# A convolution kernel with a new order of its first two groups and of its transition, and copies of k's rows in four parts

## The chip, the cores and the metric

The kernel runs on one core of one Trainium2 chip. The metric is the device time of one execution in microseconds; 356.31 us is the median of three runs of the kernel before (354.74 to 356.72).

## The reference, cut to what matters

For each of 32 batches there is an x of 64 heads and 1024 steps. Stage one makes for each head a kernel of 1024 taps out of 64 complex exponentials, convolves the masked x with it causally, adds a skip term and adds the result to x. Stage two multiplies each batch by the 1024 x 1024 matrix of its own adapter (ids 3 to 7) and adds that too.

```python
P = dtA[:, :, None] * jnp.arange(length)
K = 2.0 * jnp.einsum('hn,hnl->hl', Cs, jnp.exp(P)).real
...
y = irfft(rfft(u_m, n=2*L) * rfft(K, n=2*L))[..., :L] + u_m * D[:, None]
x = x + y * mask[:, None, :]
w = weight[adapter_ids]
x = x + jnp.einsum('bsi,boi->bso', x, w)
```

## The kernel before, in words

The heads form 8 groups of 8; a group has 4 pairs. For each group g:
- VectorE makes angles (`angles`), ScalarE their sines (`sines`), VectorE multiplies them with magnitudes (`factors`), ScalarE swaps halves (`exchange`), GpSimd makes `left` (`left_factor`), and TensorE multiplies it out to the group's k (`k_rows_made`). `k_high` on ScalarE and `k_low` on VectorE split k into two 16-bit parts, and ScalarE's queue stores them as `k_row` (`store_k`, 32 KB).
- SP copies each row of `k_row` 32 times with padding into `k_padded` (`copy_rows`, 1152 KB a group; in group 0 `copy_first_rows`, 288 KB a pair), and reads from there, shifted by one step per partition, two strips of 512 KB for each pair (`load_strips`). A pair's strips may be loaded when the pair one group before has been convolved.
- For x, ScalarE sums magnitudes (`sum_x`), TensorE adds them over partitions (`sum_x_bound`), VectorE makes a power of two (`x_scales`), and ScalarE and VectorE make two 16-bit parts (`x_high`, `x_low`).
- TensorE convolves a pair in two halves of 24 matmuls (`convolve`, L1135); between the halves it may do a group's `k_rows_made`. VectorE scales and masks the result into `mid` (`mask_pair`), GpSimd adds it to z (`add_masked`). `mid` holds two pairs.

A slot of stage two is up to two batches with one adapter: z_hi and z_lo of both, w_hi and w_lo of the adapter in four quarters. For the first slot SP loads the quarters behind the last strips, GpSimd adds the identity (`add_identity`, L509), ScalarE makes w_hi (L656), VectorE w_lo (L1022), each quarter by quarter; TensorE multiplies in `first_slot` (L1201), later slots at L1235. Between the last pair and `first_slot` lies the transition: the last pairs' results must be in z_hi and z_lo first (`high_parts`, `low_parts`, and a short way of its own for the last pair).

The order of work on each engine is written out by hand: groups 0 and 1 straight, groups 2 to 4 in a loop, then the rest. Each engine works through its list in order and waits on semaphores (`k_stored`, `k_copied`, `conv_done`, `masked`, `added` and so on); SP's list is the order of the transfers too.

## Time and profile before

| | us |
|---|---|
| median of 3 runs | 356.31 |
| the profiled execution | 354.95 |
| its span | 353.2 |
| TensorE busy, matmuls | 310.4 (88%) |
| VectorE busy | 215.2 (61%) |
| ScalarE busy | 151.7 (43%) |
| GpSimd busy | 118.7 (34%) |
| mean of the DMA rate over the span | 231 GB/s |

The profile is of one execution. Its times start at the first instruction; between its span and its time lie 1.8 us. A row of the timeline merges like instructions that follow each other, and the count of matmuls can be twice that of the program where data are plain f32. PE is TensorE, DVE VectorE, ACT ScalarE, POOL GpSimd; SPq is SP's queue. The granted clock is 1.00 but for stretches after idle times of TensorE.

### The profile page before, as it was taken

The page shows a single profiled execution, that of the slowest core. Times are in us where ns is not written, and L with a number is a line of the kernel's source. Part 1 is how long each engine was busy: PE and PEld are TensorE (multiplying, and loading weights), DVE is VectorE, ACT ScalarE, POOL GpSimd, SP SyncE. Part 2 cuts the span into 40 slices and gives each one's busy share as a digit, 9 for nine tenths or more (in the row PEclk, how much of TensorE's full clock was granted, in tenths as well). Part 3 has the DMA queues.
Part 4 walks back from the last instruction along what each step waited for, and adds up shares of the span by engine and source line. Part 5 has one row for each costly group of instructions (what it writes and reads, how often), then busy time and mean ns, then how long its engine had stood idle before and what let it go on. Part 6 is the DMA issues. An engine that isn't in the chain of part 4 may idle for free.

```text
span 353.2 us, 8212 instructions
## 1 busy us (share of the span) xinstructions
PE 310.4 (88%) x2604; PEld 272.7 (77%) x2605; DVE 215.2 (61%) x352; ACT 151.7 (43%) x210; POOL 118.7 (34%) x133
## 2 busy tenths in 40 slices
PE   0049789499999999977999999999999999999993
PEld 0049679498989999976888888888888888888882
DVE  5979987559889667669637740963312873196200
ACT  1956474824346501037508532653331753473200
POOL 4022665346596662565005301810001600250000
PEclk9999999969999999998999999999999999999999
DMA  7986899969999999991187038612227623932222
GB/s 260 354 367 187 320 350 392 398 248 337 376 368 389 401 366 405 399 415 50 24 307 267 0 90 312 226 27 62 59 59 291 243 59 77 401 116 59 59 60 61
DMA packets 20602, 81.60 MB, mean 231 GB/s; under 512 B 4512, under 2 KB 4704, under 8 KB 16992
## 3 DMA queue, kind: packets, MB, share of 16 engines
q1 hardware_dynamic: 18320, 80.98, 62.6%
q10 hardware_dynamic: 2256, 0.30, 0.5%
q8 instruction: 14, 0.23, 0.2%
q14 instruction: 12, 0.10, 0.1%
HBM read 72.58 MB, written 18.64 MB: 258 GB/s over the span
## 4 chain that ended last, share of the span: by engine, by line
PE 70%; DVE 15%; DMA 5%; issue 4%; ACT 3%; DVEq 1%; SPq 0%; ACTq 0%
PE bank L1235 49%; PE bank L1135 15%; PE bank L1201 4%; DMA strips<-k_padded 3%; ACT magnitude L592 2%; DMA k_row<-k_tile 2%; DVE turns L766 2%; DVE mid L842 1%; DVE phase L767 1%; DVE phase L760 1%; PE bank L1116 1%; DVE factor L778 1%; DVE z_lo L1027 1%; DVE scratch L729 1%; DMA small<-in_params 1%
## 5 line engine op out<-in xcount | busy, mean ns | idle before, releaser
L1135 PE MATMUL bank<-x,strips 128*128 (+8 forms) x1536 | 102.4, 228 | 2.1 <-DMA strips<-k_padded 2.1
L1135 PEld LDWEIGHTS bank<-x,strips 128*128 128x128 f16 x1536 | 98.4, 99 | 5.6 <-DMA strips<-k_padded 1.8
L509 POOL TENSOR_TENSOR w_raw<-w_raw,ident 128x128 f32<-128x128 f32 x40 | 40.4, 1033 | 118.5 <-DMA w_raw<-in_w 105.6
L1235 PE MATMUL bank<-w_hi,z_lo 128*128 128x512 f32 x256 | 78.8, 389 | 0.0
L1235 PE MATMUL bank<-w_hi,z_hi 128*128 128x512 f32 x256 | 78.8, 389 | 0.0
L1235 PE MATMUL bank<-w_lo,z_hi 128*128 128x512 f32 x256 | 78.7, 389 | 0.0
L487 POOL TENSOR_TENSOR z<-z,mid 128x512 f32 (+1 forms) x31 | 46.3, 1505 | 41.6 <-DVE mid L842 41.5
L1027 DVE TENSOR_TENSOR z_lo<-z,z_hi 128x512 fp32r<-128x512 f32 (+2 forms) x36 | 37.2, 1073 | 34.6 <-ACT z_hi L661 34.5
L1235 PEld LDWEIGHTS bank<-w_hi,z_hi 128*128 128x128 f32 x256 | 48.0, 188 | 10.0
L1235 PEld LDWEIGHTS bank<-w_hi,z_lo 128*128 128x128 f32 x256 | 48.0, 188 | 10.0
L1235 PEld LDWEIGHTS bank<-w_lo,z_hi 128*128 128x128 f32 x256 | 48.0, 188 | 9.9
L1022 DVE TENSOR_TENSOR w_lo<-w_raw,w_hi 128x2048 fp32r<-128x2048 f32 x20 | 48.0, 2448 | 4.7 <-ACT w_hi L656 4.7
L661 ACT CAST z_hi<-z 128x512 fp32r (+2 forms) x36 | 36.9, 1073 | 31.7 <-PE bank L1135 16.8
L656 ACT CAST w_hi<-w_raw 128x2048 fp32r<-128x2048 f32 x20 | 37.8, 1910 | 16.2 <-POOL w_raw L509 8.7
L679 ACT COPY o_tile<-bank 128x512 f32<-128x512 f32 x16 | 9.4, 585 | 72.6 <-PE bank L1235 69.1
L1042 DVE COPY o_tile<-bank 128x512 f32<-128x512 f32 x16 | 11.0, 689 | 45.8 <-PE bank L1235 44.6
L842 DVE SCALAR_TENSOR_TENSOR mid<-bank,small,mask 128x256 f32<-128x256 f32 x64 | 27.4, 475 | 16.4 <-PE bank L1135 14.5
L1146 PE MATMUL bank<-small,ones 128*128 128x4 f32 x16 | 3.4, 283 | 25.9 <-ACT magnitude L592 25.9
L601 ACT ACTIVATE x<-z,small 128x2048 f16<-128x2048 f32 (+1 forms) x8 | 16.0, 2001 | 18.7 <-PE bank L1135 14.5
L471 POOL COPY skip_row<-small 1x8 f32<-1x8 f32 (+1 forms) x8 | 12.7, 1587 | 32.5 <-DVE factor L778 32.5
L1146 PEld LDWEIGHTS bank<-small,ones 128*128 128x128 f32 x16 | 2.8, 219 | 26.1 <-issue 20.9
L829 DVE SCALAR_TENSOR_TENSOR x<-z,small,x 128x2048 f16<-128x2048 f32 (+1 forms) x8 | 21.8, 2729 | 1.2 <-ACT x L601 1.2
(175 smaller groups left out, 220.3 us busy)
## 6 DMA issues: line engine op xcount, KB each, us to landing
strips<-k_padded SPq DMA_DIRECT2D x64, 512.0 KB, 6.9
w_raw<-in_w SPq DMA_DIRECT2D x20, 1024.0 KB, 8.6
out<-o_tile SPq DMA_DIRECT2D x34, 256.0 KB
z<-in_x SPq DMA_DIRECT2D x8, 1024.0 KB, 5.4
k_padded<-k_row SPq DMA_DIRECT2D x7, 1152.0 KB, 8.3
k_padded<-k_row SPq DMA_DIRECT2D x4, 288.0 KB, 3.9
k_row<-k_tile ACTq DMA_DIRECT2D x8, 32.0 KB, 6.7
small<-in_params SPq DMA_DIRECT2D x1, 192.0 KB, 2.5
```

What stands on the lines that cost most here:

```text
L487: nc.gpsimd.tensor_tensor(z_pair[:, bass.ds(n, 1)].rearrange("p o e n -> p (o e n)"), z_pair[:, bass.ds(n, 1)].rearrange("p o e n -> p (o ...
L509: nc.gpsimd.tensor_tensor(diagonal, diagonal, ident[:, :], ALU.add).then_inc(diag_ready, 1)
L601: nc.scalar.activation(x16[:, bass.ds(g % 2, 1), 0, :].rearrange("p o n -> p (o n)"), z_group[:, bass.ds(g, 1), :].rearrange("p o n -> p ( ...
L656: nc.scalar.copy(w_hi[:, cs, :].rearrange("p c n -> p (c n)"), raw(q).rearrange("p c n -> p (c n)")).then_inc(w_hi_ready, 1)
L661: nc.scalar.copy(z_hi[:, par, :, j * H + channels.start:j * H + channels.stop], z_hcb[:, :, channels, bass.ds(b[j], 1)].rearrange("p c h o ...
L829: v.scalar_tensor_tensor(buffer[:, 1, :], z_group[:, bass.ds(g, 1), :].rearrange("p o n -> p (o n)"), x_scale[:, bass.ds(g, 1)], buffer[:, ...
L842: v.scalar_tensor_tensor(mid[:, k % 2, e, :], conv_ps[k][:, e * COL:(e + 1) * COL], xk_inverse[:, bass.ds(2 * n + e, 1)], mask[:, :, :].re ...
L1022: v.tensor_tensor(w_lo[:, cs, :], raw(q), w_hi[:, cs, :].bitcast(f32), ALU.subtract).then_inc(w_lo_ready, 1)
L1027: v.tensor_tensor(z_lo[:, par, :, j * H + channels.start:j * H + channels.stop], z_hcb[:, :, channels, bass.ds(b[j], 1)].rearrange("p c h ...
L1135: last = mm(conv_ps[k][:, e * COL + d * B:(e + 1) * COL], strips16[:, k, e, k_part, d, :], x16[:, bass.ds(g % 2, 1), x_part, col:col + (NB ...
L1201: last = mm(slot_ps[0][half][:, :], left_[:, 0, c, :], right[:, c, half * HALF:(half + 1) * HALF], start=(start and c == CQ * q and left_ ...
L1235: last = mm(slot_ps[par][half][:, :], left_[:, par, c, :], right[:, c, half * HALF:(half + 1) * HALF], start=(c == 0 and left_ is z_hi and ...
```

## The change

In groups 0 and 1 the work of TensorE, ScalarE, VectorE and SP comes in another order. k's rows of each group are copied in four parts, one for each pair, and from group 2 on each part stands behind the strips of the same pair of the group before. Two activations of one column each are added on ScalarE, which load the table of the sine. The four instructions on the adapter ids move behind the loop on VectorE. In the transition the last pair but one takes the short way too (`split_late`), GpSimd adds the identity to the first quarter before it adds pair (7,2), TensorE multiplies nine times with `ident` before the first slot, and takes w_lo of the third quarter before w_hi of the fourth.

```diff
@@ -60,7 +60,7 @@
...
     F_B0, F_B1, F_FIRST, F_ADAPTER, F_TWO, F_ACTIVE, F_NUMBER, F_ODD = range(FIELDS)
-    WARM_START, WARM_SECOND = 26, 16
+    WARM_START, WARM_SECOND, WARM_MIDDLE = 26, 16, 9
     PEEL = 4
...
     SCALED = 3
@@ -317,25 +317,18 @@
...
-            def copy_rows(g):
+            def copy_rows_of_pair(g, k):
                 sp.wait_ge(k_stored, 16 * (g + 1))
-                sp.dma_start(k_dram[g * GH:(g + 1) * GH].rearrange("h q n -> q h n"),
-                             k_row[g * GH:(g + 1) * GH].unsqueeze(0).to_broadcast([COPIES, GH, KROW])
-                             ).then_inc(k_copied, 16)
-
-            def copy_first_rows(k):
-
-                sp.wait_ge(k_stored, 16)
-                sp.dma_start(k_dram[2 * k:2 * k + 2].rearrange("h q n -> q h n"),
-                             k_row[2 * k:2 * k + 2].unsqueeze(0).to_broadcast([COPIES, 2, KROW])
-                             ).then_inc(first_copied[k], 16)
+                h = g * GH + 2 * k
+                sp.dma_start(k_dram[h:h + 2].rearrange("h q n -> q h n"),
+                             k_row[h:h + 2].unsqueeze(0).to_broadcast([COPIES, 2, KROW])
+                             ).then_inc(pair_copied[k], 16)
...
-                if g == 0:
-                    sp.wait_ge(first_copied[k], 16)
-                else:
+                sp.wait_ge(pair_copied[k], 16 * (g + 1))
+                if g > 0:
...
                 for e in range(2):
@@ -351,17 +344,20 @@
...
             for k in range(NPAIR):
-                copy_first_rows(k)
-            for g in range(NG - 1):
-                if g > 0:
-
-                    sp.wait_ge(k_copied, 16 * g)
+                copy_rows_of_pair(0, k)
+            for k in range(NPAIR):
+                load_strips(0, k)
+            for k in range(NPAIR):
+                copy_rows_of_pair(1, k)
+            for k in range(NPAIR):
+                load_strips(1, k)
+                for late in ((), (0, 1), (2,), (3,))[k]:
+                    copy_rows_of_pair(2, late)
+            for g in range(2, NG - 1):
                 for k in range(NPAIR):
                     load_strips(g, k)
-                    if k == (2 if g == 0 else 1):
-                        copy_rows(g + 1)
-
-            sp.wait_ge(k_copied, 16 * (NG - 1))
+                    copy_rows_of_pair(g + 1, k)
+
             for k in range(NPAIR):
@@ -511,8 +507,12 @@
             add_masked(NG - 2)
-            add_masked(NG - 1, [0, 1, 2])
-            add_identity(0)
+            add_masked(NG - 1, [0, 1])
+            add_identity(0, [0])
+
+            pool.wait_ge(late_lo_ready, 1)
+            add_masked(NG - 1, [2])
+            add_identity(0, [1, 2, 3])
...
                 first = field(pool, s, F_FIRST, 1)
@@ -610,6 +610,8 @@
...
             scaled_magnitudes(2)
+            act.wait_ge(coef_ready, 2)
+            nc.scalar.activation(sin2[:, 0:1], angle2[:, 0:1], ACT.Sin)
             k_high(0)
...
             sines(1)
@@ -625,12 +627,13 @@
...
             rest_of_magnitudes()
+            nc.scalar.activation(sin2[:, 0:1], angle2[:, 0:1], ACT.Sin)
             exchange(3)
...
             store_k(3)
+            sines(4)
             x_high(2)
-            sines(4)
             exchange(4)
...
             k_high(4)
@@ -698,12 +701,14 @@
...
             act.wait_ge(added, (NG - 1) * NPAIR)
-            act.wait_ge(conv_done, (NG - 1) * NPAIR + 2)
+            act.wait_ge(conv_done, (NG - 1) * NPAIR + 1)
             high_parts(first_slot, 0, slice(0, H - GH), early_hi_ready)
+            act.wait_ge(added, NG * NPAIR - 2)
+            high_parts(first_slot, 0, slice(H - GH, H - 4), z_hi_ready)
+            split_high(0)
+
             act.wait_ge(added, NG * NPAIR - 1)
-            high_parts(first_slot, 0, slice(H - GH, H - 2), z_hi_ready)
-            split_high(0)
             act.wait_ge(added_last, 1)
...
             last_slot(act, finish_last)
@@ -948,8 +953,8 @@
...
             angles(4)
+            mask_pair(1, 0)
             k_low(3)
-            mask_pair(1, 0)
             x_scales(2)
...
             factors(4)
@@ -959,17 +964,16 @@
...
-            link(v.tensor_scalar(wrap, ids_i, 0.0, float(NA), ALU.is_lt, ALU.mult))
-            link(v.tensor_tensor(ids, ids_i, wrap, ALU.add))
-            link(v.tensor_scalar(ids, ids, 0.0, NA - 1.0, ALU.max, ALU.min))
-            v.tensor_reduce(least_adapter, ids[0:1, 0:B], AX, ALU.min).then_inc(least_ready, 1)
-
             with dve.Fori(2, NG - 3) as g:
...
+            link(v.tensor_scalar(wrap, ids_i, 0.0, float(NA), ALU.is_lt, ALU.mult))
+            link(v.tensor_tensor(ids, ids_i, wrap, ALU.add))
+            link(v.tensor_scalar(ids, ids, 0.0, NA - 1.0, ALU.max, ALU.min))
+            v.tensor_reduce(least_adapter, ids[0:1, 0:B], AX, ALU.min).then_inc(least_ready, 1)
...
             link(v.tensor_tensor(same, same, below, ALU.mult))
@@ -1066,30 +1070,39 @@
...
             dve.wait_ge(early_hi_ready, 2)
+            low_parts(first_slot, 0, slice(0, H - GH), early_lo_ready)
+
+            def split_late(k):
+
+
+                heads = slice(H - GH + 2 * k, H - GH + 2 * k + 2)
+
+                def late(part):
+                    return part[:, 0, :, :].rearrange("p c (j h) -> p j c h", j=2)[:, :, :, heads]
+
+                dve.wait_ge(masked, 2 * ((NG - 1) * NPAIR + k + 1))
+                dve.wait_ge(x_loaded, NG)
+                if k == NPAIR - 1:
+                    dve.wait_ge(late_lo_ready, 1)
+                for j in range(2):
+                    chain.mark(v.tensor_tensor(late_slices[:, j, :, :].unsqueeze(3),
+                                               z_hcb[:, :, heads, bass.ds(first_slot[j], 1)],
+                                               mid[:, k % 2, :, :].rearrange("p e (c b) -> p c e b", c=NB)[:, :, :, bass.ds(first_slot[j], 1)],
+                                               ALU.add))
+                dve.wait_ge(dve_step, chain.n)
+                v.tensor_copy(late(z_hi), late_slices[:, :, :, :]).then_inc(late_hi_ready, 1)
+                dve.wait_ge(late_hi_ready, k - 1)
+                v.tensor_tensor(late(z_lo), late_slices[:, :, :, :], late(z_hi).bitcast(f32),
+                                ALU.subtract).then_inc(late_lo_ready, 1)
+
             mask_pair(NG - 1, 2)
-            low_parts(first_slot, 0, slice(0, H - GH), early_lo_ready)
+            split_late(2)
             dve.wait_ge(z_hi_ready, 2)
-            low_parts(first_slot, 0, slice(H - GH, H - 2), z_lo_ready)
+            low_parts(first_slot, 0, slice(H - GH, H - 4), z_lo_ready)
             mask_pair(NG - 1, NPAIR - 1)
-            dve.wait_ge(masked, 2 * NG * NPAIR)
-            dve.wait_ge(x_loaded, NG)
-            last_mid = mid[:, (NPAIR - 1) % 2, :, :]
-            for j in range(2):
-                chain.mark(v.tensor_tensor(last_pair_first_slot[:, j, :, :].unsqueeze(3),
-                                           z_hcb[:, :, H - 2:H, bass.ds(first_slot[j], 1)],
-                                           last_mid.rearrange("p e (c b) -> p c e b", c=NB)[:, :, :, bass.ds(first_slot[j], 1)],
-                                           ALU.add))
-            dve.wait_ge(dve_step, chain.n)
-
-            def last_pair_of(part):
-                return part[:, 0, :, :].rearrange("p c (j h) -> p j c h", j=2)[:, :, :, H - 2:H]
-
-            v.tensor_copy(last_pair_of(z_hi), last_pair_first_slot[:, :, :, :]).then_inc(last_hi_ready, 1)
-            dve.wait_ge(last_hi_ready, 1)
-            v.tensor_tensor(last_pair_of(z_lo), last_pair_first_slot[:, :, :, :], last_pair_of(z_hi).bitcast(f32),
-                            ALU.subtract).then_inc(last_lo_ready, 1)
+            split_late(NPAIR - 1)
             last_pair = z_pair[:, H // 2 - 1, :, :].rearrange("p e n -> p (e n)")
-            v.tensor_tensor(last_pair, last_pair, last_mid.rearrange("p e n -> p (e n)"),
+            v.tensor_tensor(last_pair, last_pair, mid[:, (NPAIR - 1) % 2, :, :].rearrange("p e n -> p (e n)"),
                             ALU.add).then_inc(added_last, 1)
             for q in range(Q):
@@ -1160,16 +1173,16 @@
...
             sum_x_bound(1)
-            k_rows_made(2)
-            convolve(0, 1)
+            convolve(0, 1, lambda: k_rows_made(2))
             convolve(0, 2)
             convolve(0, 3)
-            convolve(1, 0, lambda: k_rows_made(3))
+            convolve(1, 0)
+            convolve(1, 1, lambda: k_rows_made(3))
             sum_x_bound(2)
-            convolve(1, 1)
             convolve(1, 2)
+            convolve(1, 3)
+            k_rows_made(4)
             sum_x_bound(3)
-            convolve(1, 3, lambda: k_rows_made(4))
             with pe.Fori(2, NG - 3) as g:
...
                 convolve(g, 1)
@@ -1216,8 +1229,8 @@
...
                 with_low(1)
+                with_low(2)
                 with_high(3)
-                with_low(2)
                 with_low(3, stop=True)
             def slot(s, par, t):
@@ -1240,10 +1253,12 @@
             pe.wait_ge(table_ready, 1)
+            for _ in range(WARM_MIDDLE):
+                mm(banks[5][:, 0:P], ident[:, :], ident[:, :], start=True, stop=True)
             pe.wait_ge(masked, 2 * NG * NPAIR)
...
             pe.wait_ge(z_lo_ready, 2)
-            pe.wait_ge(last_lo_ready, 1)
+            pe.wait_ge(late_lo_ready, 2)
             first_slot()
```

SP from the copies of group 0 on, before; `k_padded` is the copied k, `strips` what TensorE reads:

```order
L330 DMA k_padded<-k_row 32x2x1152 x4
L342 DMA strips<-k_padded 128x1x1024 x6
L323 DMA k_padded<-k_row 32x8x1152
L342 DMA strips<-k_padded 128x1x1024 x6
L323 DMA k_padded<-k_row 32x8x1152
L342 DMA strips<-k_padded 128x1x1024 x8
```

One copy of 8 rows stands behind two or three pairs of strips. And of the change:

```order
L324 DMA k_padded<-k_row 32x2x1152 x4
L335 DMA strips<-k_padded 128x1x1024 x8
L324 DMA k_padded<-k_row 32x2x1152 x4
L335 DMA strips<-k_padded 128x1x1024 x4
L324 DMA k_padded<-k_row 32x2x1152 x2
L335 DMA strips<-k_padded 128x1x1024 x2
L324 DMA k_padded<-k_row 32x2x1152
L335 DMA strips<-k_padded 128x1x1024 x2
L324 DMA k_padded<-k_row 32x2x1152
```

The strips of the last pair of group 0 stand ahead of the copies of group 1, all four copies of group 1 ahead of its first strips, and from there on parts and pairs of strips alternate.

ScalarE from the exponentials of the magnitudes to the sine of group 4, before; `x` is the 16-bit x, `swapped` the exchange:

```order
L541 ACT_TABLE_LOAD
L541 ACTIVATE mag<-mag 128x2x1280
L565 COPY swapped<-factor 64x256
L566 COPY swapped<-factor 64x256
L592 ACTIVATE magnitude,small<-z 128x512 x4
L577 CAST k_tile<-bank 32x256
L581 DMA k_row<-k_tile 32x8x32
L601 ACTIVATE x<-z,small 128x2048
L556 ACT_TABLE_LOAD
L556 ACTIVATE sine<-phase,small 128x512
```

The table load for the sine stands right before it. And of the change:

```order
L541 ACT_TABLE_LOAD
L541 ACTIVATE mag<-mag 128x2x1280
L630 ACT_TABLE_LOAD
L630 ACTIVATE small<-small 128x1
L565 COPY swapped<-factor 64x256
L566 COPY swapped<-factor 64x256
L592 ACTIVATE magnitude,small<-z 128x512 x4
L577 CAST k_tile<-bank 32x256
L581 DMA k_row<-k_tile 32x8x32
L556 ACTIVATE sine<-phase,small 128x512
L601 ACTIVATE x<-z,small 128x2048
```

The table load stands before the exchange of group 3, and the sine before x of group 2.

GpSimd at the end of the convolutions, before; `w_raw` is the weights as loaded, to whose diagonal blocks the identity is added:

```order
L487 TENSOR_TENSOR z<-z,mid 128x512 x12
L509 TENSOR_TENSOR w_raw<-w_raw,ident 128x128 x8
```

All additions to z come first. And of the change:

```order
L483 TENSOR_TENSOR z<-z,mid 128x512 x11
L505 TENSOR_TENSOR w_raw<-w_raw,ident 128x128 x2
L483 TENSOR_TENSOR z<-z,mid 128x512
L505 TENSOR_TENSOR w_raw<-w_raw,ident 128x128 x6
```

One addition to z moved behind the first quarter of the identity.

## Rows read from the trace of the kernel before

**Rows 1.** The page, DMA issues: what, queue, count, KB each, median us to landing
```profile
k_padded<-k_row SPq DMA_DIRECT2D x7, 1152.0 KB, 8.3
...
k_row<-k_tile ACTq DMA_DIRECT2D x8, 32.0 KB, 6.7
```

**Rows 2.** Timeline of TensorE: start us, us, instruction, idle before it and its releaser
```profile
43.39 0.69 PE L1116 MATMUL bank<-factor,left 128*32 128x32 f32 x16 [2.02 <-POOL left L480]
...
52.05 4.75 PE L1135 MATMUL bank<-x,strips 128*128 128x256 f16 x72 [1.71 <-DMA strips<-k_padded]
...
62.72 3.21 PE L1135 MATMUL bank<-x,strips 128*128 128x256 f16 x48 [0.35 <-DMA strips<-k_padded]
...
70.39 0.59 PE L1146 MATMUL bank<-small,ones 128*128 128x4 f32 x2 [4.47 <-ACT magnitude L592]
...
86.84 0.38 PE L1146 MATMUL bank<-small,ones 128*128 128x4 f32 x2 [0.58 <-ACT magnitude L592]
...
101.00 0.38 PE L1146 MATMUL bank<-small,ones 128*128 128x4 f32 x2 [0.56 <-ACT magnitude L592]
```

**Rows 3.** Timeline of SP, the queue that issues copies and strips
```profile
27.69 2.63 SPq L330 DMA_DIRECT2D k_padded<-k_row  x4
...
42.50 0.60 SPq L323 DMA_DIRECT2D k_padded<-k_row  x1
...
54.05 9.77 SPq L342 DMA_DIRECT2D strips<-k_padded  x8
...
97.41 1.16 SPq L342 DMA_DIRECT2D strips<-k_padded  x2
...
98.63 0.60 SPq L323 DMA_DIRECT2D k_padded<-k_row  x1
```

**Rows 4.** DMAs to landing: the four parts, two strips, one copy of 98.63
```profile
DMA to landing us min/median/max: 3.3/3.9/4.8
...
DMA to landing us min/median/max: 5.3/5.7/6.1
...
k_padded<-k_row SPq DMA_DIRECT2D x1, 1152.0 KB, 8.4
```

**Rows 5.** Timelines of ScalarE and GpSimd between 25 and 68 us
```profile
25.05 0.48 ACT L577 CAST k_tile<-k_scaled 32x256 f16<-32x256 f32 x1 [1.28 <-DVE k_scaled L784]
...
53.47 0.40 ACT L565 COPY swapped<-factor 64x256 f32<-64x256 f32 x1 [1.67 <-DVE factor L778]
...
55.14 0.73 POOL L480 TENSOR_TENSOR left<-left,swapped 128x256 f32<-128x256 f32 x1
...
62.13 2.00 ACT L601 ACTIVATE x<-z,small 128x2048 f16<-128x2048 f32 x1 [4.19 <-DVE small L822]
...
67.78 0.63 ACT L592 ACTIVATE magnitude<-z 128x512 f32<-128x512 f32 x1
```

**Rows 6.** Window view: stretch, us, busy time of each engine, granted clock, DMA
```profile
91.30:105.40 14.10, 13.54 (x214) 12.95 (x214) 12.35 (x21) 6.54 (x13) 9.81 (x9) 1.00 0.99 369
...
144.00:157.00 13.00, 12.89 (x208) 12.52 (x205) 7.81 (x21) 1.99 (x3) 7.13 (x6) 1.00 1.02 404
```

**Rows 7.** Timelines of TensorE, VectorE, GpSimd in the transition
```profile
160.69 0.70 PE L1201 MATMUL bank<-w_hi,z_hi 128*128 128x512 f32 x2 [3.80 <-DVE z_lo L1089]
...
165.12 0.63 PE L1201 MATMUL bank<-w_hi,z_hi 128*128 128x512 f32 x2
...
173.31 0.61 PE L1235 MATMUL bank<-w_hi,z_hi 128*128 128x512 f32 x2
...
160.96 9.43 DVE L1022 TENSOR_TENSOR w_lo<-w_raw,w_hi 128x2048 fp32r<-128x2048 f32 x4
...
170.31 2.07 DVE L1027 TENSOR_TENSOR z_lo<-z,z_hi 128x512 fp32r<-128x512 f32 x2
...
159.31 0.87 POOL L509 TENSOR_TENSOR w_raw<-w_raw,ident 128x128 f32<-128x128 f32 x2 [0.29 <-SPq L390]
...
162.44 3.60 POOL L509 TENSOR_TENSOR w_raw<-w_raw,ident 128x128 f32<-128x128 f32 x2 [2.27 <-SPq L390]
```

6 lines of the change are left out of this document (3 added, 3 removed).

## The prediction

> **What bounds the kernel now.** Read first the table of DMA issues [rows 1] and two stretches of the window view, then the engines' timelines from 24 to 92 us and from 144 to 174 us. From 173.3 us to the end TensorE multiplies without a gap worth naming (768 matmuls, 49% of the chain of waits), and nothing in the change touches those slots. So what counts is how early the first matmul of slot 1 starts, today at 173.31 [rows 7].
>
> Two things stand before it. The convolutions run as a train of 32 pairs, 3.2 us each. In groups 2 to 4 a group takes 14.15 us, read between the sums before the last pair (from 86.84 to 101.00) [rows 2]. Before that the train is ragged: 2.02 us waiting for `left`, 1.71 and 0.35 us for strips, 4.47 us for the sums of magnitudes [rows 2]. And the DMA engines are nearly as full as TensorE: share 0.99 at 369 GB/s in a steady group, 1.02 at 404 GB/s at the end of the phase [rows 6]. Whoever moves TensorE earlier must ask whether the transfers can follow.
>
> **The queue's prices.** All strips, copies and weights go through SP's one queue and land in order of issue. Two strips issued at 97.41 and 0.56 later land 5.3 and 6.1 us later, 1.3 us apart; the copy issued behind them at 98.63 lands 8.4 us later, at 107.0, so its turn took 3.0 us [rows 4, 3]. A steady group is 8 x 1.28 + 3.0 = 13.2 us of queue against 14.15 of TensorE: 0.9 us of slack.
>
> **Part 1: copies in four parts.** Today one copy of 1152 KB stands in the queue behind two pairs of strips; now four of 288 KB, each behind a pair. What one part costs in a full queue no row shows. Below: a quarter of the whole copy, 3.0 / 4 = 0.74 us. Above: the four parts of group 0, which land 3.3 to 4.8 us after issues from 27.69 to 29.7, that is from 31.0 to 34.5: 3.5 us for three, 1.17 each [rows 4, 3]. Those had an empty queue ahead and were issued 0.66 apart, so they aren't a clean reading of a full one; I take 0.85, nearer the quarter, since each still consists of whole padded rows of 4608 bytes, and keep both ends. SP's issues: three more of 0.6 us a group (four took 2.63 at 27.69, one takes 0.60 [rows 3]), 7 a group with the eight of the strips, within 14.15; covered.
>
> The Trainium skill, "DMA: Bandwidth & Descriptors" (Anatomy of one DMA; Rules for kernel authors), speaks against this part: a DMA has about 2.0 us of fixed cost beside its bytes, and 1 MiB or more per DMA is what reaches full bandwidth. If that fixed part stood in the queue, a part would take, as an estimate from that page, 2.7 us and the kernel would lose tens of us; strips of 512 KB landing 1.3 us apart [rows 4] show that here it overlaps with the neighbours.
>
> **Part 2: the start, groups 0 and 1.** (a) Strips of the last pair of group 0 stood behind the copy of group 1, which waits for the store of k's rows until 42.50; they are now issued right behind the six others, which go out from 31.0 at about 0.65 us each, so at 35 [rows 3]. With 1.28 a strip they land by about 47.2 (my estimate: the ten parts and strips before them end at 44.6). The 1.71 us wait goes. (b) k's rows of group 2 go between the halves of pair (0,1): half a pair (1.6 us) fills the 2.02 us wait for `left`, which still comes at 43.3. (c) Rows of group 3 move from pair (1,0) into (1,1), since `left` ends only at 55.87 [rows 5] and TensorE is now ahead. (d) Sines of group 4 come before `x_high(2)`, and their table is loaded ahead, behind the exponentials of the magnitudes, where ScalarE waits for VectorE's factors anyway (1.67 us, until 53.47). That takes 1.28 + 0.72 us out of the chain 62.13 (`x_high`) to 67.78 (sums) [rows 5]. (e) The sum of group 3 moves behind pair (1,3) and k's rows, so TensorE has 3.2 + 0.7 us more work before it. (f) The same trick at 23.8 puts 1.28 + about 0.2 us into the 1.28 us of idle time before `k_high(0)` at 25.05 [rows 5]: costs 0.2 us of the start, my estimate.
>
> The new schedule, by these durations: (0,0) 37.3 to 40.5; sum 41.0; (0,1) with rows 41.3 to 45.6; (0,2) 48.8; (0,3) 52.0; (1,0) 55.2; (1,1) with rows 59.1; sum 59.4; (1,2) has its strips when it asks (today issued from 54.05 and late by 0.35 at 62.72; now copies of group 1 end 47.2 + 3.4, and eight strips and two parts later, about 60, both strips of (1,2) are there), to 63; (1,3) 66.2; rows 66.9. The sum of group 3 needs: sum of group 2 at 59.4, scale 1.6, `x_high` 2.0, exchange 0.9, magnitudes 2.6: 66.5. So it no longer makes TensorE wait, and group 2 starts at about 67.2; today it starts at 86.84 - 9.7 = 77.1.
> What is late next is a transfer. The copies of group 3 wait for the store of its rows, issued at 59 where VectorE's `k_low(3)` comes, landing 6.7 us later [rows 1] (7 to 8 under load), at 66; behind the first of them stand the strips of pair (2,1), which land at about 71.3 (0.7 us of issue, 4 us at least to land) where TensorE wants them at 70.4. So the sum before (2,3), today at 86.84, comes at 67.2 + 0.9 + 9.6 = 77.7: TensorE is 9.0 us ahead.
>
> **Part 3: can the queue follow?** From the second strip of (2,1), landing at 72.5, the queue still has 44 strips, 19 parts, and the four quarters of the first weights (4.2 MB at 404 GB/s [rows 6], with landing about 11 us): 72.5 + 44 x 1.28 + 19 x 0.85 + 11 = 156.0. Today the last quarter is there at 162.4, as VectorE's neighbour GpSimd shows by starting on it at 162.44 [rows 7]. So the weights gain 6.4 us, less than TensorE's 9.0: the queue sets the end.
>
> **Part 4: the transition.** Today TensorE idles 3.80 us, falls to the lower of its two clock levels and pays it back until 165.12: 12 matmuls in 4.43 us where the later ones take 0.23 each, 1.7 us lost [rows 7]. The nine matmuls on `ident` fill about 2.2 us of the hole, so the remaining idle is near 1 us, like the 2.02 after which no clock fell. Pair (7,2) is split early by VectorE, whose last-pair work then starts up to 1 us sooner. But none of this decides: slot 1 needs its z_lo, and that comes after four w_lo subtractions from 160.96 and 2.07 us more, to 172.4 [rows 7], with 0.9 us of slack to 173.31. The last w_lo needs the last quarter: from its arrival 162.44 to the end of z_lo are 9.9 us. With the quarter at 156.0: 165.9, plus 0.2 to start, 166.1. That is 7.2 us before 173.31. I take off 0.3 for GpSimd's additions of the identity, below.
>
> **Sum.** 7.2 - 0.3 = 6.9 us, (f) being inside the queue's rounding. The profiled execution took 354.95 us (span 353.2), so 348.1. It lies 1.4 below the median of the runs, 356.31, and about 1.0 below their mean; on the middle of the two the forecast is **349.1 us**. Bounds by the part's price: at 0.74 the gain is 9.0 (346.9), at 1.17 it is 0.8 (355.1).
>
> **Rivals.**
> 1. *The parts are dear, the queue eats the gain.* For: shares 0.99 to 1.02, and 1.17 us a part at the start. Against: equal packets, and the margin of 0.9 us a group. At 1.0 a part: 19 x 0.15 = 2.9 less, 352; at 1.17: 355. Chance 0.16.
> 2. *Slower: the queue turns from follower to brake.* Parts alternating with strips could cost more than either alone. With 28 parts, and 2 us of the hole at 67 us as a cushion, the gain is gone at about 1.2 us a part and each further 0.1 costs 2 to 2.8 us: at 1.3, 19 x 0.1 + 9 x 0.1 = 2.8 over, 359. The place would be strips waits in groups 3 to 6, today none. Chance 0.05. The fixed cost of the skill's page "DMA: Bandwidth & Descriptors" (Anatomy of one DMA) would be this case at its extreme.
> 3. *GpSimd's last identity falls behind two w_lo instructions.* Its two additions on the last quarter took 3.60 us beside w_lo, where the two at 159.31 took 0.87 [rows 7]. If both are caught, w_hi of the last quarter and all behind it come 1.4 later: 350.5. It depends on phase. Chance 0.12.
> 4. *The start gains only half,* because a store of k's rows lands late and SP holds strips of group 1 or 2 behind it. Then 352. Chance 0.08.
> 5. *The change of the start doesn't act:* the chain through VectorE's angles sets 67 to 78 us in any order: within 1.5 us of before. The order takes a table load and a wait out of that chain, against it. Chance 0.03.
> The forecast itself, 346.5 to 351: 0.56.
>
> **Range and chances.** 345.5 to 353.5 holds the forecast, rivals 3 and 4 and half of 1. What a measurement here can tell from no change is 0.5%, 1.8 us. Faster: forecast, 3, 4, and three quarters of 1: 0.88. Same: the rest of 1 and 5: 0.07. Slower: 0.05.
>
> **What would show it.** Right: the sum before (2,3) near 78; one wait on strips of about 1 us there and none later; parts landing 0.8 to 0.9 apart from their neighbours; the last quarter of the first weights near 156; granted clock 1.00 through the transition; slot 1 at about 166. Wrong: waits on strips in groups 3 to 6 (rivals 1, 2); w_hi of the last quarter more than 4.5 us behind its arrival (rival 3); SP holding strips of group 2 for a store beyond 67 us (rival 4); the sum before (2,3) later than 84 (rival 5).

## The result and the profile after

| | before | after |
|---|---|---|
| median, us | 355.52 (352.1 to 356.72) | 349.79 (347.79 to 350.69) |
| ratio | | 0.985, 95% interval 0.9802 to 0.9898 |
| the profiled execution, its span | 354.95, 353.2 | 349.68, 348.0 |
| first convolution | 37.29 | 39.47 |
| sum before the last pair of group 2 | 86.84 | 82.32 |
| last convolution ends | 156.89 | 152.54 |
| last quarter of the first weights lands | 162.37 | 157.45 |
| slot 1 starts | 173.31 | 167.70 |

The kernel is 1.5% faster, 349.8 us against 349.1 forecast. The landmarks are starts and ends of rows, and for transfers issue plus time to landing. The sum of a group is TensorE's row on `small,ones` that adds the magnitudes of that group's x: the sum of group 3 is the last before group 2, the sum of group 4 before pair (2,3). Medians and ranges here and below are of all executions, while the ratios leave out single ones over 1.5% above the fastest of their kernel: one of the kernel with strips ahead, which is the one profiled, one of that with SP's order alone, and one of that with strips ahead and one addition. The page after, its groups (busy us, mean ns of one, then idle us before it and its releaser) and its DMA issues:

```profile
L1148 PE MATMUL bank<-x,strips 128*128 (+8 forms) x1536 | 101.4, 226 | 8.2 <-DMA strips<-k_padded 8.0
strips<-k_padded SPq DMA_DIRECT2D x64, 512.0 KB, 8.5
k_padded<-k_row SPq DMA_DIRECT2D x32, 288.0 KB, 8.2
```

The 32 parts stand where seven whole copies and four parts stood in [rows 1]. TensorE now waits 8.0 us for strips in all, where it waited 2.1. Its timeline, answering to [rows 2] and [rows 7]:

```profile
39.47 3.21 PE L1148 MATMUL bank<-x,strips 128*128 128x256 f16 x48 [2.12 <-DMA strips<-k_padded]
...
44.36 0.69 PE L1129 MATMUL bank<-factor,left 128*32 128x32 f32 x16
...
53.76 1.68 PE L1148 MATMUL bank<-x,strips 128*128 128x256 f16 x24 [0.93 <-DMA strips<-k_padded]
56.06 3.22 PE L1148 MATMUL bank<-x,strips 128*128 128x256 f16 x48 [0.62 <-DMA strips<-k_padded]
...
69.42 0.39 PE L1159 MATMUL bank<-small,ones 128*128 128x4 f32 x2
...
74.23 1.71 PE L1148 MATMUL bank<-x,strips 128*128 x24 [1.36 <-DMA strips<-k_padded]
77.09 1.71 PE L1148 MATMUL bank<-x,strips 128*128 x24 [1.15 <-DMA strips<-k_padded]
...
82.32 0.36 PE L1159 MATMUL bank<-small,ones 128*128 128x4 f32 x2
...
90.46 6.57 PE L1148 MATMUL bank<-x,strips 128*128 x96 [0.89 <-DMA strips<-k_padded]
...
152.39 2.25 PE L1257 MATMUL bank<-ident 128*128 128x128 f32 x18
155.48 0.70 PE L1214 MATMUL bank<-w_hi,z_hi 128*128 128x512 f32 x2 [0.84 <-DVE z_lo L1095]
...
167.70 0.73 PE L1248 MATMUL bank<-w_hi,z_hi 128*128 128x512 f32 x2 [0.22 <-DVE z_lo L1031]
```

Gone are the 2.02 us for `left` (the rows now start at 44.36 with no idle before them), the 1.71 us for strips of (0,3) and the 4.47 us for magnitudes (69.42, no idle). New are waits for strips in groups 1 and 2, and one of 0.89 us in group 3. In the transition the idle time is 0.84 us instead of 3.80.

The prediction names the wait of 4.47 us before the sum of group 3, but not what it did to the clock. Of before, around that sum and one group later:

```profile
70.84 3.04 PE L1135 MATMUL bank<-x,strips 128*128 128x256 f16 x24
...
74.88 11.38 PE L1135 MATMUL bank<-x,strips 128*128 128x256 f16 x168
...
87.17 1.74 PE L1135 MATMUL bank<-x,strips 128*128 x24
...
89.57 10.87 PE L1135 MATMUL bank<-x,strips 128*128 x168
```
```profile
66.00:77.00 11.00, 6.61 (x69) 5.96 (x70) 6.32 (x15) 3.97 (x12) 6.41 (x6) 0.69 0.86 343
```

The granted clock was 0.69 over these 11 us. The same work, from the sum to the end of 168 matmuls, took 15.87 us there (70.39 to 86.26) and 13.60 one group later (86.84 to 100.44). So 2.3 of the 4.5 us by which the sum of group 4 comes earlier are the clock, which in after is at full speed from 28.9 us to 346.3.

SP's queue around the strips of pair (2,1), as [rows 3]:

```profile
60.24 1.17 SPq L335 DMA_DIRECT2D strips<-k_padded  x2
68.88 0.60 SPq L324 DMA_DIRECT2D k_padded<-k_row  x1
69.58 1.19 SPq L335 DMA_DIRECT2D strips<-k_padded  x2
...
DMA to landing us min/median/max: 4.4/5.6/6.8
```

SP stands from 61.4 to 68.88, until the rows of group 3 are stored. The two strips issued at 69.58 and 0.6 later land 4.4 and 6.8 us later, at 74.0 and 77.0, just before the two rows of TensorE that wait for them. The window view of a steady group and of the end of the phase, as [rows 6]:

```profile
88.50:102.50 14.00, 13.01 (x209) 12.52 (x208) 11.37 (x21) 6.02 (x14) 9.30 (x8) 1.00 1.03 417
144.00:157.00 13.00, 12.16 (x163) 11.57 (x162) 10.11 (x22) 6.67 (x7) 8.34 (x11) 1.00 0.92 370
```

This stretch now moves 417 GB/s, before 369. That is 5.8 MB in 14 us, more than the 5.4 MB of one group's strips and copies: the queue works off a backlog. That SP has something under way all the time is not new, it holds from 31 us to the last of the first weights in both kernels. VectorE, ScalarE and GpSimd in the transition, as [rows 7]:

```profile
156.02 9.68 DVE L1026 TENSOR_TENSOR w_lo<-w_raw,w_hi 128x2048 fp32r<-128x2048 f32 x4
165.63 2.01 DVE L1031 TENSOR_TENSOR z_lo<-z,z_hi 128x512 fp32r<-128x512 f32 x2
...
161.39 1.92 ACT L659 CAST w_hi<-w_raw 128x2048 fp32r<-128x2048 f32 x1 [3.02 <-POOL w_raw L505]
...
155.09 1.32 POOL L505 TENSOR_TENSOR w_raw<-w_raw,ident 128x128 f32<-128x128 f32 x2 [0.88 <-SPq L386]
157.52 3.84 POOL L505 TENSOR_TENSOR w_raw<-w_raw,ident 128x128 f32<-128x128 f32 x2 [1.10 <-SPq L386]
```

The four w_lo stand in one row without a gap, 2.42 us each, behind the last work on the convolutions. The last w_hi ends at 163.3, when VectorE is just done with the third w_lo (156.02 + 3 x 2.42 = 163.3): weights and VectorE arrive together.

### The profile page after: what moved, and what is told of

The parts are those of the page before. It is cut to its first block, busy times and chain, and to the rows that moved or that the text cites. A ratio compares the mean times of both kernels' runs of the same rounds, so it can differ in the third digit from the quotient of the medians.

```text
span 348.0 us, 8299 instructions
## 1 busy us (share of the span) xinstructions
PE 309.4 (89%) x2622; PEld 271.9 (78%) x2623; DVE 215.3 (62%) x356; ACT 152.0 (44%) x212; POOL 113.8 (33%) x133
## 4 chain that ended last, share of the span: by engine, by line
PE 50%; DVE 1%; issue 0%; DVEq 0%
PE bank L1248 50%; DVE z_lo L1031 0%; DVE o_tile L1063 0%; DVEq L1062 0%
## 5 line engine op out<-in xcount | busy, mean ns | idle before, releaser
L1248 PE MATMUL bank<-w_hi,z_hi 128*128 128x512 f32 x256 | 78.9, 389 | 0.2 <-DVE z_lo L1031 0.2
L1248 PE MATMUL bank<-w_hi,z_lo 128*128 128x512 f32 x256 | 78.9, 389 | 0.0
L505 POOL TENSOR_TENSOR w_raw<-w_raw,ident 128x128 f32<-128x128 f32 x40 | 37.7, 964 | 121.4 <-DMA w_raw<-in_w 110.0
L483 POOL TENSOR_TENSOR z<-z,mid 128x512 f32 (+1 forms) x31 | 43.9, 1428 | 39.7 <-DVE mid L847 38.5
L834 DVE SCALAR_TENSOR_TENSOR x<-z,small,x 128x2048 f16<-128x2048 f32 (+1 forms) x8 | 22.6, 2826 | 2.8 <-ACT x L601 2.5
L467 POOL COPY skip_row<-small 1x8 f32<-1x8 f32 (+1 forms) x8 | 11.3, 1411 | 30.7 <-DVE factor L783 30.7
L592 ACT ACTIVATE magnitude<-z 128x512 f32<-128x512 f32 (+1 forms) x32 | 19.7, 617 | 0.2
```

The costliest lines, as they stand in the source:

```text
L483: nc.gpsimd.tensor_tensor(z_pair[:, bass.ds(n, 1)].rearrange("p o e n -> p (o e n)"), z_pair[:, bass.ds(n, 1)].rearrange("p o e n -> p (o ...
L505: nc.gpsimd.tensor_tensor(diagonal, diagonal, ident[:, :], ALU.add).then_inc(diag_ready, 1)
L592: nc.scalar.activation(magnitude[:, k, :], z_pair[:, bass.ds(g * NPAIR + k, 1)].rearrange("p o e n -> p (o e n)"), ACT.Abs, accum_out=x_su ...
L834: v.scalar_tensor_tensor(buffer[:, 1, :], z_group[:, bass.ds(g, 1), :].rearrange("p o n -> p (o n)"), x_scale[:, bass.ds(g, 1)], buffer[:, ...
L1248: last = mm(slot_ps[par][half][:, :], left_[:, par, c, :], right[:, c, half * HALF:(half + 1) * HALF], start=(c == 0 and left_ is z_hi and ...
```

## The experiments

The theory after the result: the gain is TensorE's lead over before, won in groups 0 to 2 and carried to the end, and the parts give nothing of their own. Rivals: the parts close gaps of the queue; or the transition carries the gain.

**Which piece of the change.** Three pieces can be exchanged one by one: SP's order with the parts, the order of the other engines in groups 0 and 1, and the transition. First the transition alone; of its diff against before:

```diff
-            add_masked(NG - 1, [0, 1, 2])
-            add_identity(0)
+            add_masked(NG - 1, [0, 1])
+            add_identity(0, [0])
+
+            pool.wait_ge(late_lo_ready, 1)
+            add_masked(NG - 1, [2])
+            add_identity(0, [1, 2, 3])
...
+            for _ in range(WARM_MIDDLE):
+                mm(banks[5][:, 0:P], ident[:, :], ident[:, :], start=True, stop=True)
```

> The kernel before with only the new transition (early split of pair (7,2), identity of the first quarter ahead, nine matmuls on ident, w_lo of quarter 2 before w_hi of quarter 3). Theory (slot 1 hangs on the arrival of the last quarter of the first weights, 9.9 us ahead of z_lo): the clock stays at 1.00 and the first slot ends earlier, but slot 1 starts at most 0.9 us earlier (the slack of TensorE today), 353.2 to 352.3 of span. Rival (the start of the first slot and the clock set it): 1.2 + 1.7 = 2.9 us earlier.

Measured: 354.93 us (353.63 to 356.55), ratio 0.9984 (0.9953 to 1.0015): no gain that can be told. In the profiled execution TensorE idles only 0.84 us before the first slot and the convolutions end 1.05 us earlier than before, but slot 1 starts only 0.22 us earlier: it ran into the trap described under "The transition" below. And all of the change but the transition, against after:

```diff
-                with_low(2)
                 with_high(3)
+                with_low(2)
...
-            for _ in range(WARM_MIDDLE):
-                mm(banks[5][:, 0:P], ident[:, :], ident[:, :], start=True, stop=True)
```

> The changed kernel with the transition of before. Theory: slot 1 starts 0.9 us later than in the changed kernel, relative to the arrival of the last quarter; the span is 348.9. Rival: 2.9 us later, 350.9.

Measured: 350.92 us (348.73 to 353.53), ratio 0.9884 (0.9849 to 0.9919). The gain comes from the start. In the profiles slot 1 stands 11.42 us behind the last quarter with the old transition and 10.25 with the new one: 1.2 us, nearer the theory's 0.9 than the rival's 2.9. Then SP's order and whole copies of before, with the rest of the change, against after:

```diff
-                    copy_rows_of_pair(g + 1, k)
+                    if k == (2 if g == 0 else 1):
+                        copy_rows(g + 1)
```

> The changed kernel with SP's order and copies of before: one whole copy a group, the strips of pair (0,3) behind the copy of group 1; the new order of the other engines and the new transition stay. Theory (the strips of (0,3) 8 us earlier and the sum of group 3 off the path each give a part): the wait of about 1.7 us on the strips of (0,3) is back and those of (1,2) too, 2 to 3 us; the wait of 1.6 us on the store before (2,1) is not. The sum before (2,3) comes at about 84, the end 2 us later than the changed kernel's, 0.990 of before. Rival (SP's order is the whole gain): like before, 0.998.

Measured: 350.07 us (349.12 to 351.74), ratio 0.9859 (0.982 to 0.9898), as good as the whole change. The expectation missed: the sum of group 4 stands at 81.38 and not at 84. Its TensorE:

```profile
63.34 6.26 PE L1152 MATMUL bank<-x,strips 128*128 128x256 f16 x96 [1.79 <-DMA strips<-k_padded]
...
70.19 0.39 PE L1163 MATMUL bank<-small,ones 128*128 128x4 f32 x2
...
81.38 0.38 PE L1163 MATMUL bank<-small,ones 128*128 128x4 f32 x2 [1.51 <-ACT magnitude L596]
```

It waits for strips in group 1 and for none in group 2, whose strips stand ahead of the copy there. The other way round, before with SP's new order and the parts alone:

```diff
-                    if k == (2 if g == 0 else 1):
-                        copy_rows(g + 1)
+                    copy_rows_of_pair(g + 1, k)
```

> The kernel before with SP's new order and the copies in parts alone; the engines' order and the transition stay as before. Theory A (the start's gain comes from the order of TensorE, ScalarE and VectorE, and SP's order only follows it): k's rows of group 2 are stored when they were before, so the sum of group 3 stands at 69 to 71 us and the one of group 4 at 85 to 87 (before 86.84, after 82.32); median 354 to 356, ratio 0.997 to 1.003. Theory B (SP's order gives a good part of it, and the kernel with the old SP order kept its gain by another way): the sum of group 4 at 83 to 84 us, ratio 0.988 to 0.993.

Measured: 354.18 us (352.73 to 358.19), ratio 0.9954 (0.9922 to 0.9986), the sum of group 4 at 84.81. Between the two theories, nearer A. Its TensorE waits for no strip but for what the engines' order makes late:

```profile
43.38 0.69 PE L1112 MATMUL bank<-factor,left 128*32 128x32 f32 x16 [2.01 <-POOL left L476]
...
56.29 0.69 PE L1112 MATMUL bank<-factor,left 128*32 128x32 f32 x16 [1.38 <-POOL left L476]
...
69.36 0.58 PE L1142 MATMUL bank<-small,ones 128*128 128x4 f32 x2 [4.37 <-ACT magnitude L588]
...
84.81 0.38 PE L1142 MATMUL bank<-small,ones 128*128 128x4 f32 x2 [0.60 <-ACT magnitude L588]
```

So the order of TensorE, ScalarE and VectorE carries most: from the transition alone (0.9984) to the transition with that order (0.9859) are 1.3%; SP's order on top of it moves nothing that can be told (0.985), and alone it gives 0.5%. The 4.37 us of waiting in the last fence still pull the clock down: from that sum to the end of 168 matmuls are 14.85 us. Which of the moves on TensorE, VectorE and ScalarE does how much was not taken apart.

**What a part costs.** Whole copies from group 2 on, against after:

```diff
-                    copy_rows_of_pair(g + 1, k)
+                    if k == 1:
+                        copy_rows(g + 1)
```

> The changed kernel with one whole copy for each group from group 2 on, behind the strips of the second pair, as before the change; groups 0 and 1 stay in parts. Theory (a part costs the queue exactly a quarter, 0.75 us, so splitting as such neither gains nor loses; but the first part of group 3 stands before the strips of (2,1), and the whole copy behind them): the hole at 70 us is one pair later, the waits on strips in group 2 shrink from 2.95 us to about 1.5, the end is 0 to 1.5 us earlier than the changed kernel's. Rival (parts are cheaper or the alternation helps the strips): the end is 1 us or more later.

Measured: 349.56 us (348.74 to 352.21), ratio 0.985 (0.9806 to 0.9894). Strips are waited for 2.8 us in all, all of it before the first convolution (the forecast left 1.5 in group 2), and the median doesn't move. And twice the parts from group 3 on, the second copy into a tensor that nothing reads:

```diff
+                if g >= 3:
+                    sp.dma_start(k_twice[h:h + 2].rearrange("h q n -> q h n"),
+                                 k_row[h:h + 2].unsqueeze(0).to_broadcast([COPIES, 2, KROW])
+                                 ).then_inc(k_copied, 16)
```

> The changed kernel, but from group 3 on each part of the copies is made twice, the second time into DRAM that nobody reads: 20 more DMAs of 288 KB, nothing left out. It measures the price of a part in the full queue and how near the queue is to being the bound. Theory (a part takes 0.75 us; the queue is full from 73 us on and was 1.4 us behind TensorE at its end): parts land 0.75 us apart, 15 us of queue are added, TensorE waits on strips in groups 3 to 6, and the last weights and the end come 12 to 14 us later than the changed kernel's: 362 to 364. Rival (0.9 us of slack in each steady group): 15 - 5 x 0.9 = 10 us later, 360. Rival 2 of the prediction (1.2 us a part in alternation): 24 us of queue, 370 and more.

Measured: 364.91 us (363.67 to 367.46), ratio 1.0263 (1.0212 to 1.0313). Its last convolution ends where the row on `ident` starts:

```profile
167.49 2.25 PE L1263 MATMUL bank<-ident 128*128 128x128 f32 x18
```

That is 15.1 us behind after's 152.39, for 20 parts: 0.755 us a part, a quarter of the whole copy's 3.0. It is no clean division, since this execution also took 4.76 us for its first pair of 48 matmuls, at the lower clock, where after took 3.21. The landings bear it out: in this profile and in after's a part lands 0.75 us behind the transfer before it (median of 19), and a second copy 0.70 (median of 20). The queue has no slack for 20 more, and no fixed price for each shows. The medians are 15.1 us apart too, a little over the 12 to 14 expected.

**What holds group 2.** The strips of pairs (2,1) and (2,2) ahead of the copies that wait for the store of group 3, against after:

```diff
-            for g in range(2, NG - 1):
+            for step in ((0,), (1,), (2,), (-1,), (-2,), (3,), (-3,), (-4,)):
+                if step[0] >= 0:
+                    load_strips(2, step[0])
+                else:
+                    copy_rows_of_pair(3, -step[0] - 1)
+            for g in range(3, NG - 1):
```

> The changed kernel, but in group 2 SP loads the strips of pairs 1 and 2 before it waits for the store of k's rows of group 3; the copies follow. Theory (a hole in the queue at 70 us holds back everything behind it): the strips of pair (2,1) are issued at about 62 instead of 69.6, the waits of TensorE on strips in group 2 (1.36 + 1.15 + 0.44 us) go, the sum before pair (2,3) comes at 80.7 instead of 82.3, where ScalarE's sums of magnitudes, ending at 80.67, become the last; the end comes 1.6 us earlier, 0.995 of the changed kernel, 0.98 of before. Rival 1 (TensorE's waits alone set the end): 2.9 us earlier. Rival 2 (from group 3 on the engines' own chain sets the pace in any case): sum before (2,3) earlier, but the end unchanged within 0.5 us.

Measured: 350.12 us (347.17 to 354.58), ratio 0.9853 (0.9798 to 0.9907). The strip waits of group 2 are gone, and between the sums of groups 3 and 4 lie 11.4 us instead of 12.9; then the magnitudes are the wait:

```profile
83.11 0.38 PE L1164 MATMUL bank<-small,ones 128*128 128x4 f32 x2 [1.81 <-ACT magnitude L597]
```

Yet the median is the same, where the theory had 1.6 us. The profiled execution is no guide to it: at 354.58 us it was the slowest of six. What it shows is a late start, a fall of the clock there and again after these 1.81 us (24 matmuls take 3.05 us), and the trap of the transition; start and transition have runs below. Which of them the other five executions had is not on record. Without the two Sin activations that bring the table load forward, against after:

```diff
-            act.wait_ge(coef_ready, 2)
-            nc.scalar.activation(sin2[:, 0:1], angle2[:, 0:1], ACT.Sin)
...
-            nc.scalar.activation(sin2[:, 0:1], angle2[:, 0:1], ACT.Sin)
```

> The changed kernel without the two one-column Sin activations on ScalarE that bring the table load forward. The table loads (1.28 us each) then stand in front of the sines they serve. If ScalarE is behind in groups 0 to 3 (sum of group 4 waits for its magnitudes or its rows), k's rows of group 1 or 3 are stored 1.3 us later and the median rises 0.5 to 1.3 us, ratio to the kernel before 0.987 to 0.989. Rival: the queue and the strips' landing set the pace there, the stores have over 1.3 us to spare; median within 0.5 us of the changed kernel's 349.8, ratio 0.983 to 0.987.

Measured: 350.91 us (349.28 to 351.92), ratio 0.9866 (0.9829 to 0.9902), 1.1 us above the changed kernel by the medians, but the intervals overlap: not settled.

**The start.** Its first store of k's rows lands at very different times. Issued at 26.0 to 26.2, to landing in before, in after and in the kernel with strips ahead:

```profile
DMA to landing us min/median/max: 1.6/1.6/1.6
```
```profile
DMA to landing us min/median/max: 3.3/3.3/3.3
```
```profile
DMA to landing us min/median/max: 5.2/5.2/5.2
```

The first convolution follows at 37.29, 39.47 and 41.21. In the third the clock fell after TensorE had idled 3.80 us; its TensorE and the window of 5 us from there:

```profile
41.21 4.69 PE L1153 MATMUL bank<-x,strips 128*128 128x256 f16 x48 [3.80 <-DMA strips<-k_padded]
```
```profile
41.20:46.20 5.00, 4.99 (x52) 4.60 (x53) 2.49 (x3) 0.00 (x0) 2.12 (x3) 0.66 1.02 416
```

The pair takes 4.69 us instead of 3.21. In thirteen of the fourteen profiles the store lands 0.2 to 1.1 us behind the last load of x issued before it, which was still under way on SP's queue. In the other one (all but the transition) the loads had landed at 25.8, before the store was issued, and it took 1.6 us. So the last group of x was loaded later, behind group 3's strips:

```diff
-            for g in range(NG):
+            for g in range(NG - 1):
                 sp.dma_start(z_group[:, g, :], x_in[g]).then_inc(x_arrived[g % 2], 16)
...
+                if g in (3, 4):
+                    last_x(g - 3)
```

> The changed kernel, but SP loads the last of the eight groups of x (1 MB) not at the start, but behind the strips and parts of group 3. Theory (the first store of k's rows, 32 KB, issued at 26.1, lands behind the last load of x, so its landing and the start of the convolutions vary from 37.3 us to 41.2 between executions): the first store lands at 27.6 to 28.5 in any execution, the first convolution starts at 37.2 to 38, and the end comes about 1.5 us earlier than the changed kernel's in the median, 0.981 of before, as 1 MB more in the queue behind group 3 fits into the slack of the steady groups. Rival (the queue is full from 73 us to the end, so 1 MB, 2.5 us, comes back at the end): the start is earlier, but the weights land 1 us later and the end is 1 us later.

Measured: 351.21 us (350.43 to 354.24), ratio 0.9898 (0.9853 to 0.9943). The store lands at 28.2, 0.2 us behind the load that is now the last, and the first convolution stands at 38.3. But the time is not better. The megabyte now stands in the full queue, and the profiled execution fell into the trap of the transition; how much each costs the median is not shown.

**The transition.** One addition of the identity per quarter on GpSimd, for two diagonal blocks at once, instead of one each, against after:

```diff
-                    for c in range(CQ * q, CQ * (q + 1)):
-                        diagonal = raw(q)[:, c - CQ * q, c * P:(c + 1) * P]
-                        nc.gpsimd.tensor_tensor(diagonal, diagonal,
-                                                ident[:, :], ALU.add).then_inc(diag_ready, 1)
+                    blocks = raw(q).rearrange("p c (j n) -> p (c j) n", n=P)
+                    diagonals = blocks[:, CQ * q:CQ * q + NB + 2:NB + 1, :]
+                    nc.gpsimd.tensor_tensor(diagonals, diagonals, ident[:, :].unsqueeze(1).to_broadcast([P, CQ, P]),
+                                            ALU.add).then_inc(diag_ready, CQ)
```

> The changed kernel with one addition of the identity for each quarter of the weights on GpSimd (two blocks of 128 columns in one instruction), where it takes two. Theory (an addition that meets VectorE's w_lo lasts until that instruction ends, 2.5 us, and two in a row cost 5; so slot 1 starts 10.2 to 12.4 us after the last quarter lands): it starts 9.9 to 10.4 us after in the profile, and the median is 0.8 us below the changed kernel's. Rival (VectorE's own four w_lo and two z_lo set slot 1): no change within 0.3 us.

Measured: 348.36 us (347.68 to 351.96), ratio 0.9829 (0.9782 to 0.9875): 1.4 us under after by the medians, with intervals that overlap. Slot 1 stands 10.47 us behind the last quarter, just over the 9.9 to 10.4 expected. What is called the trap here is seen where two additions a quarter meet an early w_lo. Of the kernel with whole copies, VectorE, ScalarE and GpSimd:

```profile
155.47 4.75 DVE L1037 TENSOR_TENSOR w_lo<-w_raw,w_hi 128x2048 fp32r<-128x2048 f32 x2
162.50 4.50 DVE L1037 TENSOR_TENSOR w_lo<-w_raw,w_hi 128x2048 fp32r<-128x2048 f32 x2 [2.28 <-ACT w_hi L670]
...
160.56 3.71 ACT L670 CAST w_hi<-w_raw 128x2048 fp32r<-128x2048 f32 x2 [3.94 <-POOL w_raw L516]
...
155.88 5.48 POOL L516 TENSOR_TENSOR w_raw<-w_raw,ident 128x128 f32<-128x128 f32 x4 [1.20 <-SPq L397]
```

The additions on the third quarter begin at 155.88, just after the first w_lo, and each of the first two lasts as long as a w_lo beside it. w_hi of the third quarter comes at 160.56, and VectorE stands 2.28 us. If w_lo starts later than the additions (156.02 against 155.09 in after), nothing waits. Two more kernels put the single addition together with the strips ahead, and with whole copies. The edits are those shown above.

> The changed kernel with two edits: the strips of pairs 1 and 2 of group 2 issued ahead of the copies that wait for group 3's rows, and the identity added by one GpSimd instruction a quarter instead of two. The single instruction gave 1.8 us less between the last quarter and slot 1 where the two were caught beside the lower parts' subtraction (10.5 against 12.3), and 348.4 us; the strips ahead took away the strip waits of group 2 but moved the median by nothing. Theory A (the path to the end leads over the queue, so only the transition's edit counts): 348.0 to 348.8, ratio 0.981 to 0.983. Theory B (both count where the start is early): 346.5 to 347.8, ratio 0.976 to 0.980.

> The changed kernel with whole copies of k's rows from group 2 on (one transfer of 1152 KB in place of four of 288 KB) and the identity added by one GpSimd instruction a quarter. Theory A (the parts give nothing, the single addition 1 to 2 us): 348.0 to 348.8, ratio 0.981 to 0.983, strips waited for under 3 us in all. Theory B (whole copies cost some gap in the queue that the parts close, which the other kernel hid by chance): 349 to 350.

Measured: 346.73 us (345.85 to 352.09), ratio 0.9749 (0.971 to 0.9788), and 346.86 us (345.52 to 349.22), ratio 0.9774 (0.9732 to 0.9816). By the medians that is theory B for the first, its ratio even a little lower, and for the second neither: it is faster than both. Against the same kernels with two additions (0.9853 and 0.985) the first is faster with intervals that just don't touch, the second with intervals that overlap by 0.001. TensorE, VectorE and GpSimd of the first:

```profile
78.94 0.38 PE L1164 MATMUL bank<-small,ones 128*128 128x4 f32 x2 [1.82 <-ACT magnitude L597]
...
164.02 0.74 PE L1253 MATMUL bank<-w_hi,z_hi 128*128 128x512 f32 x2 [0.22 <-DVE z_lo L1036]
...
152.59 9.43 DVE L1031 TENSOR_TENSOR w_lo<-w_raw,w_hi 128x2048 fp32r<-128x2048 f32 x4
...
153.52 1.95 POOL L510 TENSOR_TENSOR w_raw<-w_raw,ident 128x256 f32<-128x256 f32 x1 [1.71 <-SPq L391]
```

And of the second, where the additions are caught too:

```profile
151.88 9.98 DVE L1037 TENSOR_TENSOR w_lo<-w_raw,w_hi 128x2048 fp32r<-128x2048 f32 x4
...
152.31 5.19 POOL L516 TENSOR_TENSOR w_raw<-w_raw,ident 128x256 f32<-128x256 f32 x2 [1.54 <-SPq L397]
```

Two caught instructions instead of four still let w_lo run without a gap, though two of the w_lo now take 2.8 us. Both are the best kernels of this study, 8.8 to 8.9 us under before. The end of the phase in every profile, in the order of the last column:

| kernel | last convolution ends | third quarter lands | first w_lo | slot 1 | slot 1 behind first w_lo |
|---|---|---|---|---|---|
| strips ahead, one addition | 148.97 | 150.93 | 152.59 | 164.02 | 11.43 |
| no preload | 153.26 | 155.66 | 157.07 | 168.50 | 11.43 |
| one addition | 150.51 | 152.38 | 154.25 | 165.70 | 11.45 |
| after | 152.54 | 155.03 | 156.02 | 167.70 | 11.68 |
| whole copies, one addition | 149.16 | 152.18 | 151.88 | 163.84 | 11.96 |
| all but the transition | 151.50 | 154.07 | 155.59 | 167.93 | 12.34 |
| before | 156.89 | 159.24 | 160.96 | 173.31 | 12.35 |
| transition alone | 155.84 | 158.35 | 159.04 | 173.09 | 14.05 |
| old SP order | 151.41 | 153.96 | 154.60 | 168.67 | 14.07 |
| SP's order alone | 154.86 | 158.12 | 158.52 | 172.60 | 14.08 |
| parts doubled | 167.64 | 171.51 | 170.54 | 185.46 | 14.92 |
| late x | 152.45 | 155.55 | 155.22 | 170.36 | 15.14 |
| strips ahead | 154.64 | 158.04 | 157.60 | 172.74 | 15.14 |
| whole copies | 152.86 | 155.81 | 155.47 | 170.62 | 15.15 |

With two additions a quarter: where the third quarter lands 0.99 us or more ahead of the first w_lo, slot 1 follows 11.4 to 12.4 us behind it; where it lands 0.69 or less ahead, or later, 14.1 to 15.2. Each row is one execution; those of strips ahead, whole copies and parts doubled took 2.5 us or more over their kernel's median, so the table says what happens in the trap and not how often. From slot 1 to the end all fourteen take 181.6 to 182.0 us: what differs between the kernels is settled before.

## Why the prediction was right in its number and half right in its reasons

**The queue's prices, Part 1.** The price of a part, taken at 0.85, is 0.75: the lower bound was the price, and nothing of the 2.7 us that the prediction worked out for a fixed part in the queue. The start's four parts (1.17 each) were no reading of a full queue. At this price, what follows the second strip of (2,1) takes 157.45 - 76.96 = 80.5 us, forecast 83.5; 19 parts at 0.1 less are 1.9 of these 3.0. Rivals 1 and 2 fall: with whole copies the time is the same. Their sign, a wait for strips in groups 3 to 6, did come once (0.89 us at 90.46), but not by the price: the part ahead of these strips was issued at 79.17, when group 4's rows were stored, and landed 2.39 us behind its neighbour, and the kernel with one addition has no such wait. That the parts give nothing the prediction left open; whole copies show it.

**Part 2.** The steps (b), (c) and (e) did as worked out in the main: no wait for `left` at 44.36, none for magnitudes at 69.42. The first is helped by after's late start; with the new order and a first convolution at 37.0 to 38.3, 0.2 to 0.5 us of it are left in five of six profiles. (a) took away the 1.71 us, but the copies of group 1 ahead of all its strips give 0.93, 0.62 and 0.47 back. (d) is not settled; the table load and its activation end at 54.28, and the exchange starts at 54.29, 0.35 us later than VectorE's factors allow. The step that failed is the new schedule's strips of (2,1): forecast to land at 71.3 and 72.5, they landed at 74.0 and 77.0, so the sum before (2,3) stood at 82.3 and not at 77.7, a lead of 4.5 us and not 9.0. Of the missing 4.6, some 1.6 are the start: the kernel with one addition has the same program up to there, its first convolution at 38.02 and this sum at 80.68. Of the other 3.0, that kernel loses 0.9 before group 2 starts (68.11, forecast 67.2) and 2.1 at these strips, which wait in SP's list for the store of group 3's rows (68.88, forecast 66) and then take 6.8 us for the second. The clock is in the 4.5 us too: the prediction took it along unnamed, by setting its own schedule against before's 77.1. With them ahead and an early start the sum stands at 78.9, behind ScalarE's magnitudes. That is what rival 4 said, SP holding strips of group 2 for a store beyond 67 us and half of the gain at the start; I gave it 0.08. Its 352 did not come: half of a lead of 9.0 us is still 4.5, and the transition added 1.3.

**Part 3.** "The queue sets the end" was wrong, though 156.0 came near 157.45. The queue could follow. In after VectorE's four w_lo start 3.5 us behind the last convolution and have no gap; TensorE's lead of 4.5 us at (2,3) is still 4.35 at the last convolution. Even with a lead of 7.9 (strips ahead, one addition) the last quarter is there at 153.4, early enough for a w_lo row without a gap.

**Part 4.** The hole went as forecast: 0.84 us idle, and the first slot's later pairs of matmuls come every 0.45 us from the beginning. "None of this decides" was wrong. The first w_lo comes 3.48 us behind the last convolution (before 4.07), and slot 1 11.68 behind that (before 12.35): 1.26 us in all. With the lead of 4.35 that is the 5.61 us by which slot 1 is earlier, and against the transition left out the medians say 1.1, with intervals that overlap. That the profiled execution of after missed the trap, by 0.3 us of phase (0.99 us in the table, caught at 0.69), is luck; the kernel with the old SP order has the same transition and was caught.

**The sum.** Forecast 7.2 - 0.3 = 6.9 us, found 5.3 in the profiled execution (354.95 to 349.68) and 5.7 between the medians. A lead twice too large was cut by a bound of the queue that wasn't there, and the transition's gain was left out: three errors that partly cancel, so it is in part luck that 349.1 is so near.

**Rival 3.** It did not happen in after, but in seven of the fourteen profiles, and its price beside after's 11.68 is 2.4 to 3.5 us, not 1.4: the additions on the third quarter are caught as well. 0.12 was far too low. It is also the likely reason why edits on the strips (strips ahead, whole copies) showed no gain until the addition was made one: that step is worth 3.4 and 2.7 us by the medians there, and 1.4 on after. Rival 5 falls with the sum at 82.3.

What stays open: whether the preload helps, and what delays the second strip of (2,1) (2.97 us behind the first, where strips land 1.3 apart in [rows 4]). In that stretch the store of group 4's rows, issued at 71.56 on ScalarE's queue, is under way; that it is the cause is not shown.

## What to carry to other kernels

Cutting the copy in this full queue into four cost its bytes and no more, and a cut gains nothing unless something waits for a quarter of it. A train that goes ahead is carried to the end only if the hand-over behind it fits: look there for work of one engine that the earlier start of another slows down. When a table of landmarks shows two groups of differences (11.4 to 12.4, 14.1 to 15.2), settle what separates them before judging any other edit.
